# A macaron block (MoE, attention, MoE): softmax denominators from sums of the weights on POOL, and the experts' second sum added by accumulating DMAs

## The reference

```
x = X
x = x + 0.5 * moe(layernorm(x))
x = x + attention_block(layernorm(x))     # its own layernorm, and "+ its input"
x = x + 0.5 * moe(layernorm(x))

attention: Q, K, V = split(Xn @ W_in); 16 heads of 32; rope on the first 16 channels of Q and K
  probs = softmax(Q K^T / sqrt(32));  out = (probs V) @ W_out + X
moe: 64 experts, 6 for each token (from 4 of 8 groups), hidden 192, plus one shared expert
```

## Time and profile before

| | us |
|---|---|
| runs of the kernel, median of 3 | 1521.2 (1514.78 to 1522.2) |
| the profiled execution | 1513.97 |
| its span in the trace | 1512.2 |

### The profile page before, as it was taken

The page is one execution under the profiler, slowest core; times in us unless marked ns, Lnnn a source line. Parts: engine busy times, 40 slices in busy tenths (PEclk is TensorE's granted clock), DMA queues, the critical chain, the costliest instruction groups (busy, mean ns, idle before and its releaser), DMA issues.

```text
span 1512.2 us, 21658 instructions
## 1 busy us (share of the span) xinstructions
PE 1325.0 (88%) x7858; PEld 817.9 (54%) x7858; DVE 660.0 (44%) x1356; ACT 548.6 (36%) x1264; POOL 521.2 (34%) x417
## 2 busy tenths in 40 slices
PE   2999999999992588999999899989887999999990
PEld 2733666666661444554564464445433776667660
DVE  4687122222224666555654754622586222222220
ACT  1411211111111178786876886853112111111110
POOL 0321255455542742232222322200021355545544
PEclk8799999999996787999999999969998999999995
DMA  8795699999997544222532342221736799999977
GB/s 314 279 333 172 202 317 307 322 306 312 309 272 234 193 130 120 71 77 67 136 101 70 98 113 70 71 70 49 275 122 192 236 311 309 313 308 310 312 195 126
DMA packets 142826, 307.09 MB, mean 203 GB/s; under 512 B 19584, under 2 KB 30208, under 8 KB 140416
## 3 DMA queue, kind: packets, MB, share of 16 engines
q1 hardware_dynamic: 109344, 238.07, 48.9%
q0 software_dynamic: 23808, 57.69, 17.0%
q10 hardware_dynamic: 9568, 9.94, 1.9%
HBM read 222.54 MB, written 61.87 MB: 188 GB/s over the span
## 4 chain that ended last, share of the span: by engine, by line
PE 59%; DMA 16%; DVE 10%; issue 4%; POOL 4%; ACT 4%; SPq 1%; ACTq 0%; DVEq 0%; POOLq 0%
DMA buf<-xn_d,tok 10%; PE ps L355 8%; PE ps L470 6%; PE ps L414 5%; PE ps L372 5%; PE ps L285 5%; PE ps L458 4%; PE ps L359 4%; PE ps L481 4%; PE ps L426 3%; PE ps L376 3%; PE ps L340 2%; PE ps L399 2%; PE ps L299 2%; PE ps L273 2%
## 5 line engine op out<-in xcount | busy, mean ns | idle before, releaser
L355 PE MATMUL ps<-bufT,gu 128*128 128x96 f32 x2048 | 251.4, 276 | 0.5 <-ACT bufT L631 0.5
L355 PEld LDWEIGHTS ps<-bufT,gu 128*128 128x128 f32 x2048 | 240.2, 193 | 2.4 <-issue 1.6
L1133 POOL DMA_INDIRECT buf<-xn_d,tok x128 | 127.7, 998 | 300.5 <-DVE osb L968 224.0
L1037 DVE TENSOR_REDUCE Mx<-ps 128x1 f32<-128x512 f32 x256 | 168.7, 684 | 106.9 <-PE ps L426 106.4
L961 DVE TENSOR_TENSOR h<-sg,ps 128x96 f32<-128x96 f32 x128 | 32.5, 254 | 399.2 <-ACT sg L637 263.8
L671 ACT ACTIVATE ps<-ps,Mx 128x512 f32<-128x512 f32 x256 | 171.4, 670 | 46.3 <-DVE Mx L1037 41.9
L697 ACT ACTIVATE PT<-ps 128x512 f32<-128x512 f32 x256 | 152.7, 603 | 69.5 <-PE ps L458 67.8
L637 ACT ACTIVATE sg<-ps 128x192 f32<-128x192 f32 x128 | 42.3, 330 | 329.7 <-PE ps L359 314.9
L458 PE MATMUL ps<-St 98*128 98x512 f32 x256 | 123.0, 491 | 6.4 <-ACT PT L697 5.9
L372 PE MATMUL ps<-wd,h 128*96 128x512 f32 x256 | 126.3, 616 | 2.3 <-DVE hr L962 2.3
L1175 POOL TENSOR_TENSOR t<-t,rp 128x512 f32<-128x512 f32 x32 | 41.1, 1284 | 248.7 <-DVE t L1022 245.3
(11 more groups left out here) (145 smaller groups left out, 1708.8 us busy)
## 6 DMA issues: line engine op xcount, KB each, us to landing
gu<-in_L_ffn_w_gate SPq DMA_DIRECT2D x64, 768.0 KB
gu<-in_L_ffn_w_up SPq DMA_DIRECT2D x64, 768.0 KB
wd<-in_L_ffn_w_down SPq DMA_DIRECT2D x64, 512.0 KB
St<-HL SPq DMA_DIRECT2D x192, 128.0 KB, 2.3
wr<-in_L_ffn_w_down SPq DMA_DIRECT2D x128, 128.0 KB
wqk<-wqk_d SPq DMA_DIRECT2D x16, 1024.0 KB, 5.2
xn_d<-XN SPq DMA_DIRECT2D x32, 256.0 KB, 2.3
X<-in_L_attn_X SPq DMA_DIRECT2D x4, 1024.0 KB, 10.9
```

What stands on the lines that cost most here:

```text
L355: e.matmul(bk[:, CAP * j:CAP * j + CAP], w[:, c, 0:128], f.bufT[x % 3][:, c, :], start=(c == 0), stop=(c == 3))
L1037: e.tensor_reduce(Mx[:, qt, hl:hl + 1], bank((4, 5, 7)[n % 3]), AX, ALU.max, negate=True).then_inc(a_max, 1)
L1133: e.indirect_dma_start(out=f.buf[x % NB][:, :], out_offset=None, in_=f.xn_d, in_offset=bass.IndirectOffsetOnAxis(ap=f.tok[:, x:x + 1], axi ...
```

## The change

1. `act_scores`, `dve_invert`, `pe_spread`, `act_spread`, `pe_broadcast` and `dve_broadcast` are gone. The bank of a score matmul is free after DVE's maximum (`a_max`).
2. POOL adds the weights PT of each head over the four blocks of 128 keys (`pool_sum`, 12 additions of 128x512 in each unit, into four buffers Sm). PE multiplies each sum by a block of 32 columns of ones at step 6 of the next unit (`pe_denominators`, four heads side by side). DVE inverts the 128x512 result in PSUM and multiplies cT by it (`dve_normalize`).
3. An exponential may overwrite its PT buffer only when the addition that reads it is done (`added`).
4. The copies of V go from DVE to ACT, the residuals from POOL to ACT (`act_value`, `act_residual`).
5. POOL's twelve additions of Y1 go; it starts three DMAs that add `yb_d` onto X instead. The statistics of tiles 4 to 15 wait for these.
6. To make room, the projection weights wqk and the shuffle buffer t2 have one buffer each in place of two.

```diff
-        wqk = [at("wqk", AW + 8 * KB * j, [128, 2, 4, 2, 128], F32R) for j in range(2)]
+        wqk = at("wqk", AW, [128, 2, 4, 2, 128], F32R)
...
-        t2 = at("t2", o + 4 * KB, [128, 2, S])
+        t2 = at("t2", o + 4 * KB, [128, S])
...
             if n >= 3:
-                e.wait_ge(a_den, n - 2)
+                e.wait_ge(a_max, n - 2)
...
+        def pe_denominators(e, u):
+            e.wait_ge(a_sum, 12 * u + 12)
+            bk = turn(e, ("den", u), a_nrm, u + 1)
+            for hl in range(4):
+                t = e.matmul(bk[32 * hl:32 * hl + 32, :], cst[:, C_ON:C_ON + DH], Sm[hl][:, :], start=True, stop=True,
+                             tile_position=(0, 32 * hl), skip_group_check=True)
+            t.then_inc(a_den, 1)
...
+        def added(n):
+
+            u, i = n // 16, n % 16
+            return 12 * u + (i + 1 if i < 4 else i - 3)
...
-        def act_scores(e, u, j):
-            hl, qt = j // 4, j % 4
-            n = 16 * u + j
-            bk = bank((4, 5, 7)[n % 3])
-            e.wait_ge(a_max, n + 1)
-            if j == 0 and u:
-                e.wait_ge(a_inv, u)
-            e.activation(bk, bk, ACT.Exp, bias=Mx[:, qt, hl:hl + 1], accum_out=Dn[:, qt, hl:hl + 1]).then_inc(a_den, 1)
...
+        def act_value(e, i):
...
+            e.copy(V[b % 2][:, j, :], bank(has["V", i])).then_inc(a_V, 1)
+
+        def act_residual(e, i):
+            e.wait_ge(a_zh, i + 1)
+            e.activation(X[:, i, :], X[:, i, :], ACT.Identity, bias=NM[:, i:i + 1], scale=OP[:, i:i + 1]).then_inc(a_xz, 1)
...
             if n >= NP:
                 e.wait_ge(a_pv, (n - NP) // 4 + 1)
+                e.wait_ge(a_sum, added(n - NP))
             e.activation(PT[n % NP][:, :], bank(2 + j % 2), ACT.Exp).then_inc(a_exp, 1)
...
+        def dve_normalize(e, u):
+            bk = bank(has["den", u])
+            e.wait_ge(a_den, u + 1)
+            e.reciprocal(bk, bk).then_inc(a_inv, 1)
+            e.wait_ge(a_inv, u + 1)
             e.wait_ge(a_dr, u + 1)
-            e.tensor_tensor(cT[:, u % 4, :], cT[:, u % 4, :], bank(has["nrm", u]), ALU.mult).then_inc(a_nrm, 1)
+            e.tensor_tensor(cT[:, u % 4, :], cT[:, u % 4, :], bk, ALU.mult).then_inc(a_nrm, 1)
...
+        def pool_sum(e, u, i):
+
+            hl, n = i % 4, 16 * u + i
+            e.wait_ge(a_exp, n + 1)
+            if i >= 8:
+                e.wait_ge(a_sum, 12 * u + i - 7)
+            elif u:
+                e.wait_ge(a_den, u)
+            first = Sm[hl] if i >= 8 else PT[(n - 4) % NP]
+            e.tensor_tensor(Sm[hl][:, :], first[:, :], PT[n % NP][:, :], ALU.add).then_inc(a_sum, 1)
 
         def pool_attention(e):
+
+            for g in range(1, 4):
+                e.wait_ge(s_yx[g], 16)
+                e.dma_start(X[:, 4 * g:4 * g + 4, :], yb_d[512 * g:512 * g + 512, :].rearrange("(i p) d -> p i d", p=128),
+                            accum_op=ALU.add).then_inc(s_ac[g], 16)
             e.wait_ge(a_add, 4)
...
+                    if now and j >= 8:
+                        pool_sum(e, u, j - 4)
+                    if back and j < 4:
+                        pool_sum(e, u - 1, j + 12)
```

More of the change, by code:

```diff
@@ L1202, in pool_attention @@
             for u in range(-2, NU + 1):
[L1203 to L1204 removed]
+                now, far, back = 0 <= u < NU, 0 <= u + 2 < NU, 0 <= u - 1 < NU
                 for j in range(16):
[L1206 removed]
+                    if far and j in (1, 4):
                         pool_project(e, u + 2, (1, 4).index(j))
@@ L1301, in sp_attention @@
             e.dma_start(rp[:, :, :], rope).then_inc(s_rp, 16)
-            again(e, 1)
-            fetch(e, 1)
-            again(e, 2)
-            again(e, 3)
+            for g in range(1, 4):
+                again(e, g)
             for k in range(2):
```

127 lines of the change are left out of this document (38 added, 89 removed).

## The result

| | median us | ratio to before |
|---|---|---|
| before, 4 runs | 1521.7 (1514.78 to 1527.55) | |
| changed, 4 runs | 1554.5 (1547.14 to 1566.93) | 1.0226, 95% interval 1.0146 to 1.0305 |
| changed once more, 6 runs against 11 of before | 1559.19 (1545.97 to 1572.0) | 1.0266, 1.0219 to 1.0313 |

A forecast was written before the change was run, and what follows sets the result against it. PE, busy for 88% of the span, was taken to bound the kernel. The terms sum to +12.5 us, 1526.5 from the profiled 1513.97 or 1533.7 from the median 1521.2; 1530 was predicted, range 1497 to 1555.

The forecast's parts named there:

- the wait for the twelfth sum: Step 6 of a unit: PE waits 1.9 us for POOL's last addition before the denominators' product.
- rival 3: All sixteen units: the reciprocal costs 4.3 us, about 13 us more on the path, total 1543; chance 0.08.
- From unit 15 on: Units 15 and 16: reciprocals stand bare before tiles and results, 3.4 us each; +7.4 us in all (3 to 10).
- rival 2: Attention units: PE's clock falls after its new waits, ten slow stretches of nearly 2 us, +18, total 1548; chance 0.15.
- Tile units: Three units: centring queued behind the reciprocal and POOL's hold on DVE against PE's present waits; +2 us each (-5 to +6).
- Rival 1: Tile units: ACT's relief wins, about -5 us each instead of +2; total 1503; chance 0.25.
- Units 13 and 14: These two units lose ACT as their bound and get POOL's work instead; -7.5 us together (-15 to -2).
- Result units: Three units: PE waits 1.9 us for the sum and 1.9 for cT, less 0.89 saved; +2.9 us each.
- Value units: Six units: waits of 1.9 and 0.6 us against savings of 0.44, 0.06 and 0.39; +1.6 us each.
- the 0.6 for the bank: Value units: PE waits 0.6 us as the ninth maximum, behind the reciprocal, frees the twelfth score matmul's bank late.
- Start: Start and units -1 and 0: earlier statistics through accumulating DMAs, and ACT relieved; -12 us (-18 to -3).
- rival 4: Start: accumulating DMAs crawl behind weight loads and land after 520, so nothing is gained; total 1540; chance 0.12.

The follow-up runs named there:

- the kernel with the sums alone: The changed kernel with Y1 loaded whole and added by POOL as before, in place of the accumulating DMAs: 1563.47 us, 1.0315 of before.
- late product, short sums and no inversion: Changed kernel, denominators' product at step 8 except in result units, POOL's sums cut to 8 of 512 columns, constant multiplication for each reciprocal: 1484.24 us, 0.9781 of before.
- Without the inversion: The changed kernel with a multiplication by a constant in place of each of the 16 reciprocals: 1517.04 us, 0.998 of before.
- the DMAs alone: The kernel before with three accumulating DMAs in place of POOL's twelve additions of Y1, nothing else changed: 1510.75 us, 0.9953 of before.

## Why the prediction was right and wrong

- **Direction and the prices of the new instructions were right.** ACT's second exponential was hidden; the wait for the twelfth sum (1.96 us measured, 1.9 forecast), the reciprocal (3.37 and 3.35) and POOL at 22 us of 28 in a value unit (23 forecast) are as the prediction has them. The price extrapolated from rows of 4 to 24 elements held at 512, so rival 3 (4.3 us) is out; the estimate of 4.3 us worked out from the Trainium skill's repeat count (VectorE: DVE Perf Modes, First, the fixed hardware budget) is a quarter too high here. What failed is what a wait does behind itself: on PE's clock in unit 15, and in the tile units. Three slips in its working change nothing: the reciprocal's upper bound comes to 4.4 us and not 4.5, six value units at 1.61 make 9.7 and not 9.8, and the denominators' product took 1.06 us, not 0.06 less than the broadcast's 1.05.
- **From unit 15 on: +21.5 for +7.4, the step that failed most.** I priced each of the two reciprocals there by its own 3.4 us and put PE's clock behind it at nothing. Both 3.4 us are there. But behind the first PE, which had stood for 4.9 us, worked at 1.2 GHz for 28 us: +12.8 up to the unit's last exponential. The results' 1.7 and the second MoE's 2.9 more were in no term, and their cause stays open. This is rival 2. I had judged it by a tile unit that kept its clock through waits of about 1 us each; the wait here is about five times as long. Its chance (0.15) was too small. A fixed price for such a wait does not follow either, since the kernel with the sums alone lost 2.3 us there behind the same 4.86. The waits of 1.96 us, on which the rival was built, left the clock at 1.00 in value units 2, 7 and 10 and at 0.94 in 3, 6 and 11.
- **Tile units: the term was mis-sized, +4.3 on average for +2.** I had named the order (centring behind the reciprocal) and POOL's hold, but added them as a few us of delay against PE's present waits. In fact PE stood 5.4 us at one place (4.2 in unit 9), and worked at 1.2 GHz after it. Rival 1 stated its own test: a second transposition less than 1 us later. Before it stood here:

```profile
716.96 0.75 PE L386 MATMUL ps<-cst,ZH 128*128 128x128 f32 x4 [1.09 <-DVE ZH L998]
```

  It came 27.9 us behind the mark in place of 24.6, 3.3 later, so rival 1 was not right as a forecast. With the late product, short sums and no inversion a tile unit is 31.5 us, 2.8 under before, and the kernel 33 us faster than before; but that kernel leaves out work that the result needs, and no kernel with whole sums and inversions shows the gain. The hold agrees with the rule that I cited from the Trainium skill (GPSIMD Engine Reference, Key points): the multiplication with two SBUF inputs was held, 0.73 us, the one that reads PSUM was not, 0.29.
- **Units 13 and 14: -2.7 for -7.5.** The term counted ACT's relief and POOL's sums and left the reciprocal out. Without the inversion and with whole sums the two units took 48.2 us, 7.8 less than before; so it is the reciprocal that ate the gain, and POOL's sums alone leave the forecast standing. Each figure is of one trace, and the DMAs alone, which do not touch these units, have 53.0 where before has 56.0.
- **Result units: +4.2 for +2.9.** PE waits 1.96 us for the sum in all three. The first result stands 5.3 us behind the product in place of 3.7, 1.6 for the 1.9 forecast; PE's own wait for cT reads 1.88 in unit 12 but 0.54 and 0.35 in units 4 and 8, where PE was slower on the way. What is over goes with stretches at 1.2 GHz: the mean clock of the three units is 0.91, 0.95 and 0.95, before 1.00. Unit 8:

```profile
788.00:824.00 36.00, 33.14 (x127) 16.21 (x125) 19.06 (x28) 11.70 (x21) 22.20 (x19) 0.95 0.28 76
```

- **Value units: +1.9 on average for +1.6.** It is the wait; of the 0.6 for the bank hardly anything was there, and the 0.39 of a quicker `pe_weigh` did not come back in full.
- **Start: -14.4 for -12.** Of these 1.5 lie ahead of the stage: the first four tiles' statistics end at 481.0 in place of 482.6. The accumulating DMAs (KB each, median us from issue to landing) and the first statistics behind the third:

```profile
X<-yb_d POOLq DMA_DIRECT2D x3, 1024.0 KB, 20.3
```
```profile
513.72 0.69 DVE L981 BATCH_NORM_STATS2 BS<-X 128x6 f32<-128x512 f32 x1 [0.58 <-DMA X<-yb_d]
```

  The third landed at 513.7 (512 forecast), which rules out rival 4. The DMAs alone are worth 7 us in the median; the rest needs both halves.

Open stays why 2.4 GHz came back within 5 us in one trace and after 28 in two, and how a tile unit's loss divides between POOL's hold and PE's wait for the sum.

## To carry to other kernels

When an engine off the path is relieved and two others are loaded instead, price not only each new instruction but the longest gap it opens on the bounding engine, and what that engine's clock does afterwards. Look where the moved instruction stands in its engine's order: 3.4 us in front of a tile cost 3.4 and another 2 to 13 by the clock, while with unit 14's reciprocal moved to the head of unit 16 and the last one beside the shared expert's matmuls the stretch from the last mark on came within 3.4 us of before. And before splitting a long instruction into pieces, check what the pieces hold, a buffer or a bank, and where their inputs lie: beside POOL's additions the one with both inputs in SBUF took 2.5 times as long.

## What the hardware showed

- DVE's reciprocal: 3.37 us for 512 fp32 elements a partition and 0.95 for 128, the same within 0.03 us from PSUM and SBUF.
- A DVE multiplication of 128x128 beside POOL's additions: 0.73 us with both inputs in SBUF, 0.29 with one in PSUM.
- Three DMAs that add 1 MB each from DRAM onto SBUF landed 20.3 us after their issue in the median, beside loads of 6.5 MB.
- A POOL addition of 8 columns takes 0.25 us, of 512 columns 1.30.
- PE can stay at 1.2 GHz for 28 us while it is busy for 27.4 of them, with many small matmuls, behind one wait of 4.9 us (two traces of the changed kernel); in a third trace, of the sums alone, 2.4 GHz was back within 5 us of the same wait.
- Value units with a wait of 1.96 us had a mean granted clock of 1.00 (three of six) or 0.94 (three).
